# A four-stage kernel whose first stage is written out step by step, with the statistics and the application of each norm in different steps and scores ahead of projections

## The chip, the core and the metric

The kernel runs on one core of a Trainium2 chip. The time is the device time of one execution in microseconds (us). A core has five engines, each working through its own queue of instructions in order: TensorE (PE in the profile; its weight loads are listed as PEld), VectorE (DVE), ScalarE (ACT), GpSimd (POOL) and SyncE (SP, which here only issues transfers). They wait for one another by semaphores.

## What is computed

A sequence tensor x of 16 x 256 x 128 passes four residual blocks, each `x = x + LN(f(LN(x)))`. The change lies in the first one, windowed attention with sigmoid weights and 16 heads of 8:

```
x = x + _layernorm(_L0_attn_ref(_layernorm(x), wq, wkv, wo, gamma, beta))
x = x + _layernorm(_L0_ffn_ref(_layernorm(x), ...))      # attention over 16, experts
x = x + _layernorm(_L1_attn_ref(_layernorm(x), ...))     # state-space scan
x = x + _layernorm(_L1_ffn_ref(_layernorm(x), ...))      # gated ternary MLP

def _L0_attn_ref(x, wq, wkv, wo, gamma, beta):
    q = (x @ wq.T).reshape(B, T, H, HD)
    kv = (x @ wkv.T).reshape(B, T, H, 2 * HD)
    nb_k, nb_v = the 16 positions before each one
    tau = jax.nn.sigmoid(einsum('bthd,bthwd->bthw', q, nb_k) / SCALE)
    msg = einsum('bthw,bthwd->bthd', tau, nb_v)
    y = x + msg.reshape(B, T, D) @ wo.T
    return layernorm(y) * gamma + beta
```

## The kernel before

The four blocks run as stages a, b, c and d. Stage a takes the 16 sequences as 16 tiles of 256 tokens (two blocks of 128 tokens on the 128 partitions). Each engine runs `step_a(n, l, have)` for n from -2 to 16; in step n it works on several tiles at different points of their way, and `have(k)` tells whether tile n+k exists. Two sets of buffers (lanes, l = n % 2, o the other one) are used in turn, and the eight PSUM banks are four for each lane. `pipelined` (L81) writes out the first and last steps and makes a hardware loop of the twelve between them, two steps in one turn of the loop. The order of the work on each engine is the order in which `step_a` is written.

The way of one tile: DVE takes the statistics of x (`a_ln1.stats`, L109 and L112), POOL makes 1/sqrt(var+eps) of them (`rstd`, L118 and L119), DVE applies them (`apply`, L141, into t_xn). PE turns t_xn (`turn`, L1313), ACT rounds it to its high part xh (L645), DVE takes the rest as xl (L921). PE projects to q, k and v with nine matmuls of 256 columns (`project`, L1318 to L1320). ACT spreads k over four heads (hbd, L636) and copies q (mov, L652); DVE turns v and spreads it (vT and vbd, L925 and L926). PE makes the scores (L1353 lays the mask of the window, L1331 adds 32 products of 32 rows), ACT the sigmoid (tau, L657), PE the messages (L1370), ACT copies them (msgT, L664), and PE projects them out (L1337). DVE adds the residual (t_y, L948) and takes the statistics of a second norm (a_ln2) and applies it (t_zn); POOL scales and shifts it (L439, L440 into t_z); DVE takes the third norm's statistics of t_z (a_ln3) and applies it (t_o); POOL adds that to x (L465), and SP stores the tile to DRAM (L410).

In a step, PE has: project tile n+1, scores of tile n, turn tile n+2, wait for tau of tile n, its messages, wait for msgT, its outward projection. DVE has: t_y and the a_ln2 statistics of tile n-1; the a_ln1 statistics of tile n+2, a wait for POOL's `rstd` of it, its application; the application of a_ln2 (n-1); vT and vbd (n+1); the a_ln3 statistics of tile n-1, a wait for POOL's `rstd` of it, its application; and last xl of tile n+2, for which the next step's project waits.

Stage b starts when all 16 tiles are stored, and reads them back in another layout (L401). The constants and weights of all stages are loaded by ACT's queue at the start in four groups, a to d. All engines wait for group a; DVE then casts four constants, makes bqm and the high and low parts of the weights of stages a and b (`split`, L914 and L916), with a wait for group b before those of stage b, and only then begins stage a. What is printed below shows the functions that the change touches.

## Time and profile before

| | |
|---|---|
| median of 3 runs | 1067.92 us (1067.37, 1067.92, 1071.03) |
| the profiled execution | 1070.93 us |
| its span, first to last instruction | 1069.1 us |
| outside the span | 1.8 us |
| first scores of stage a (tile 0) | at 28.7 us |
| last scores of stage a (tile 15) | at 182.8 us |
| last addition of stage a | ends at 199.2 us |
| stages b, c and d | 199.2 to 1069.1 us |

The profile is of one execution. Its times are us from the first instruction unless ns stands there. A figure such as [1.09 <-POOL a_ln_rs L119] says that the engine stood idle for 1.09 us, and which instruction ended that. PEclk is TensorE's granted clock as a share of 2.4 GHz, so 0.50 is 1.2 GHz.

### The profile page before, as it was taken

Reading aid. Unit: us, or ns where it says so; the run is one execution under the profiler, and the core shown is the slowest. Engines: PE = TensorE matmul, PEld = TensorE weight load, DVE = VectorE, ACT = ScalarE, POOL = GpSimd, SP = SyncE. Lnnn points to the kernel's source line nnn. Section 1 sums busy time; section 2 is a strip of 40 time slices with the busy share of each in tenths; the row PEclk is TensorE's granted clock in tenths of the full one; section 3 lists DMA queues with packets and bytes.
Section 4 is the critical chain, followed back from the end, with each engine's and each line's share of the span. In section 5 each row is a group of like instructions: output and inputs, shape, how many; then the busy total and the mean of one; then the engine's idle time right before and its main releaser. Section 6 shows DMA issues by size and latency. Waiting matters only on the chain. (4 is left out here: it accounts for less than half of the span.)

```text
span 1069.1 us, 21886 instructions
## 1 busy us (share of the span) xinstructions
PE 876.1 (82%) x8256; PEld 721.9 (68%) x8256; DVE 683.1 (64%) x1966; ACT 556.9 (52%) x1049; POOL 460.7 (43%) x781
## 2 busy tenths in 40 slices
PE   1878777276999999998958778887669999999994
PEld 1767766265888888876745556665447878888783
DVE  3566665366588888865249999999965073370712
ACT  1434343133567667664657777778455263452630
POOL 1456565323255455434446777777660011020201
PEclk9855566555799989898878888778668999999997
DMA  9100000110000000000000000000000000000000
GB/s 311 37 12 13 15 10 17 40 50 1 2 2 2 2 2 2 2 2 1 1 1 1 1 1 1 1 1 2 1 0 1 1 1 21 1 20 1 11 11 20
DMA packets 22134, 16.55 MB, mean 15 GB/s; under 512 B 2576, under 2 KB 20376, under 8 KB 21792
## 3 DMA queue, kind: packets, MB, share of 16 engines
q1 hardware_dynamic: 17408, 8.39, 2.8%
q10 hardware_dynamic: 4640, 7.01, 1.8%
q8 instruction: 54, 0.88, 0.3%
q14 instruction: 32, 0.26, 0.1%
HBM read 11.20 MB, written 4.19 MB: 14 GB/s over the span
## 5 line engine op out<-in xcount | busy, mean ns | idle before, releaser
L118 POOL TENSOR_TENSOR d_ln_ve<-d_ln_mv,eps 128x4 f32<-128x4 f32 x16 | 3.2, 201 | 228.7 <-DVE d_ln_mv L112 228.7
L1319 PE MATMUL ps<-h_h,wh_l 128*128 128x512 f32 x256 | 99.7, 390 | 0.0
L1320 PE MATMUL ps<-h_l,wh_h 128*128 128x512 f32 x256 | 99.7, 390 | 0.0
L1318 PE MATMUL ps<-h_h,wh_h 128*128 128x512 f32 x256 | 99.7, 390 | 0.0
L1393 PE MATMUL ps<-w_e,he 128*128 128x128 f32 x512 | 87.7, 311 | 4.4 <-ACT he L676 4.0
L1331 PEld LDWEIGHTS ps<-mov,hbd 32*128 32x128 f32 x2048 | 85.2, 251 | 0.0
L1331 PE MATMUL ps<-mov,hbd 32*128 32x32 f32 (+1 forms) x2048 | 83.1, 325 | 0.0
L676 ACT ACTIVATE he<-ps,pp 128x256 f32<-128x256 f32 x128 | 59.5, 471 | 44.2 <-PE ps L1320 39.1
L1393 PEld LDWEIGHTS ps<-w_e,he 128*128 128x128 f32 x512 | 77.4, 222 | 7.0 <-ACT he L676 6.3
L1285 DVE TENSOR_TENSOR d_y<-ps,w_s 128x512 f32<-128x512 f32 x8 | 5.5, 691 | 103.0 <-PE ps L1711 103.0
L1251 DVE TENSOR_TENSOR h_l<-hid,h_h 128x512 fp32r<-128x512 f32 x64 | 48.5, 772 | 31.2 <-ACT h_h L883 30.3
L118 POOL TENSOR_TENSOR b_ln_ve<-b_ln_mv,eps 128x2 f32<-128x2 f32 x64 | 13.1, 204 | 107.8 <-DVE b_ln_mv L112 107.8
L1320 PEld LDWEIGHTS ps<-h_l,wh_h 128*128 128x128 f32 x256 | 48.1, 188 | 10.1
L1319 PEld LDWEIGHTS ps<-h_h,wh_l 128*128 128x128 f32 x256 | 48.1, 188 | 9.9
L1318 PEld LDWEIGHTS ps<-h_h,wh_h 128*128 128x128 f32 x256 | 48.1, 188 | 10.0
L1313 PE MATMUL ps<-ident,t_xn 128*128 128x128 f32 x64 | 18.4, 382 | 44.4 <-DVE t_xn L141 44.4
L887 ACT ACTIVATE hid<-ps,pp 128x512 f32<-128x512 f32 x32 | 22.1, 690 | 62.3 <-PE ps L1320 62.3
L1318 PE MATMUL ps<-hTh,we_h 128*128 128x256 f32 x128 | 53.8, 420 | 0.0
L636 ACT ACTIVATE hbd<-ps,headmask 128x256 f32<-128x256 f32 x64 | 25.1, 474 | 52.9 <-PE ps L1320 52.9
L1105 DVE TENSOR_TENSOR wall<-dec,wall 128x224 f32<-128x224 f32 (+6 forms) x112 | 47.8, 427 | 3.5
L545 POOL TENSOR_TENSOR term<-term 128x224 f32<-128x224 f32 (+2 forms) x48 | 35.4, 738 | 32.1 <-DVE term L1129 29.6
L119 POOL TENSOR_TENSOR b_ln_rs<-b_ln_ve,half 128x2 f32<-128x2 f32 x64 | 46.0, 718 | 5.0
(254 smaller groups left out, 2637.9 us busy)
## 6 DMA issues: line engine op xcount, KB each, us to landing
x<-in_x SPq DMA_DIRECT2D x16, 128.0 KB
w_h<-in_w_h ACTq DMA_DIRECT2D x2, 1024.0 KB, 7.8
x<-x SPq DMA_DIRECT2D x16, 128.0 KB, 1.8
xB<-x SPq DMA_DIRECT2D x32, 64.0 KB
out_x<-xB SPq DMA_DIRECT2D x32, 64.0 KB
w_m<-in_w_m ACTq DMA_DIRECT2D x3, 256.0 KB, 4.8
xB<-in_w_e ACTq DMA_DIRECT2D x1, 512.0 KB
w_e<-in_w_e ACTq DMA_DIRECT2D x1, 512.0 KB
```

What stands on the lines that cost most here:

```text
L119: pool.tensor_tensor(self.rs[l][:, :], self.ve[l][:, :], half[:, 0:self.k], ALU.pow).then_inc(self.rstd_ready, 1)
L545: chain.link(pool.tensor_tensor(y[:, :, j:CH], y[:, :, j:CH], wide[:, HALF - 1 - j, :, j:CH], ALU.add))
L636: last = act.activation(hbd[l][:, :, h, :], src, ACT.Copy, scale=headmask[:, h:h + 1])
L676: act.activation(he[e % 2][:, :], ps[:, HE + e % 2, 0:NT], ACT.Gelu, bias=vec("b1", e)).then_inc(he_ready, 1)
L887: act.activation(hid[l][:, m, :], bank(l, m), ACT.Gelu, scale=vec("h2_s", m)).then_inc(m_h2, 1)
L1105: ins = dve.tensor_tensor(wall[l][:, :, CH - 1 - j, j:CH], dec[l][:, 0, :, j:CH], wall[l][:, :, CH - j, j - 1:CH - 1], ALU.mult)
L1251: dve.tensor_tensor(dst[l][:, m, :], hid[l][:, m, :], high_part[l][:, m, :].bitcast(F32), ALU.subtract).then_inc(done, 1)
L1318: pe.matmul(dst, a_h, b_h, start=start, stop=True, skip_group_check=True)
L1319: pe.matmul(dst, a_l, b_h, start=False, stop=True, skip_group_check=True)
L1320: return pe.matmul(dst, a_h, b_l, start=False, stop=True, skip_group_check=True)
L1331: return pe.matmul(dst, hbd[l][heads(g), j, :, :].rearrange("p h s -> p (h s)"), mov[l][heads(g), BLK * j:BLK * j + w], start=False, stop= ...
L1393: last = pe.matmul(ps[:, ACC, P * c:P * c + P], he[e % 2][:, P * c:P * c + P], w_e2[:, e, :], start=False, stop=True, skip_group_check=True)
```

## The change

All of it concerns stage a and what lies ahead of it.

- The hardware loops of stage a on PE, ACT, DVE, POOL and SP are gone; the steps are written out, now from n = -3 to 17.
- PE: the scores of tile n stand ahead of the projection of tile n+1. The wait for xl of tile n+1 stands ahead of the scores too.
- DVE: the a_ln1 statistics are taken one step ahead of their application (for tile n+3), the a_ln3 application comes one step after its statistics (for tile n-2), and the a_ln2 application stands behind both.
- POOL: the copy of t_xn first, then `rstd` of a_ln2, the addition to x for tile n-2, scale and shift, `rstd` of a_ln1 and a_ln3 at the end.
- ACT: tau first, then hbd, xh, msgT and, last, mov.
- Group a of the loads is smaller: rows, same and negsel go to group b. DVE casts only band ahead of stage a, ACT casts rep. The splits of wf and w_e1, the casts of same and negsel, and bqm go to DVE's step 16, the wait for group b to the end of its step 14. POOL waits for group b in step 1. The Exp of log_A goes behind stage a on ACT.

```diff
-                  (wa[:, :, :], "wa"), (rows[:, :, :], "rows"), (pp[:, :], "pp")],
-            "b": [(wf[:, :, :], "wf"), ...
+                  (pp[:, :], "pp"), (wa[:, :, :], "wa")],
+            "b": [(rows[:, :, :], "rows"), (stage_f[2][:, :], "c_same"), (stage_f[3][:, :, :], "c_negsel"), (wf[:, :, :], "wf"), ...
...
 # POOL
-                if have(-1):
-                    a_ln2.rstd(pool, chain, eps, half, 1 - l, n)
-                if have(2):
-                    a_ln1.rstd(pool, chain, eps, half, l, n + 3)
...
+                if have(-2):
+                    pool.wait_ge(S["a_o"], n - 1)
+                    xt = x[:, 2 * n - 4:2 * n - 2, :]
+                    pool.tensor_tensor(xt, xt, t_o[l][:, :, :], ALU.add).then_inc(S["a_x"], 1)
...
+                    if n == 1:
+                        pool.wait_ge(w_loaded["b"], W_ALL["b"])
...
+                if have(3):
+                    a_ln1.rstd(pool, chain, eps, half, o, n + 4)
...
-            pipelined(pool, step_a, 2, 1, NB)
+            for n in range(-3, NB + 2):
+                step_a(n, n % 2, within(n))
...
 # DVE
+                if have(-2):
+                    a_ln3.apply(dve, lambda b: t_o[l][:, b, :], lambda b: t_z[l][:, b, :], l, n - 1).then_inc(S["a_o"], 1)
+                if n == NB:
+                    split(wf_h[:, :, :], wf_l[:, :, :], wf[:, 0:3, :], split_done, 2)
                 if have(-1):
                     a_ln2.apply(dve, lambda b: t_zn[o][:, b, :], lambda b: t_y[o][:, b, :], o, n).then_inc(S["a_zn"], 1)
+                if have(3):
+                    dve.wait_ge(x_loaded[o], 16 * ((n + 3) // 2 + 1))
+                    a_ln1.stats(dve, chain, lambda b: x[:, 2 * n + 6 + b, :], o)
+                if n == -3:
+                    split(wa_h[:, :, :], wa_l[:, :, :], wa[:, 0:3, :], split_done, 0)
+                if n == NB:
+                    split(we_h[:, :, :], we_l[:, :, :], w_e1[:, :, :], split_done, 4)
...
 # PE
-                if have(1):
-                    pe.wait_ge(S["a_xl"], n + 2)
-                    project(o, 4 * o, wa_h, wa_l, S["a_qk_ps"], S["a_v_ps"])
                 if have(0):
...
+                    if have(1):
+                        pe.wait_ge(S["a_xl"], n + 2)
...
+                if have(1):
+                    pe.wait_ge(S["a_xl"], n + 2)
+                    project(o, 4 * o, wa_h, wa_l, S["a_qk_ps"], S["a_v_ps"])
```

PE, a step in the middle of stage a, before (the last matmul of the projection, then the scores, the turn, the messages and the outward projection):

```order
L1320 MATMUL ps<-xl,wa_h 128x256
L1347 REGISTER_ALU
L1353 MATMUL ps<-band,rep 128x384 x4
L1331 MATMUL ps<-mov,hbd 128x48 x28
L1331 MATMUL ps<-mov,hbd 128x32 x4
L1363 REGISTER_ALU
L1311 REGISTER_ALU
L1313 MATMUL ps<-ident,t_xn 128x128 x2
L1366 ISA
L1370 MATMUL ps<-tau,vbd 32x48 x28
L1370 MATMUL ps<-tau,vbd 32x32 x4
L1337 MATMUL ps<-wa,msgT 128x128 x2
```

PE, the same step now:

```order
L1366 MATMUL ps<-band,rep 128x384 x4
L1344 MATMUL ps<-mov,hbd 128x48 x28
L1344 MATMUL ps<-mov,hbd 128x32 x4
L1331 MATMUL ps<-xh,wa_h 128x256
L1332 MATMUL ps<-xh,wa_l 128x256
L1333 MATMUL ps<-xl,wa_h 128x256
...
L1326 MATMUL ps<-ident,t_xn 128x128 x2
L1386 MATMUL ps<-tau,vbd 32x48 x28
L1386 MATMUL ps<-tau,vbd 32x32 x4
L1350 MATMUL ps<-wa,msgT 128x128 x2
```

The projection moved from ahead of the scores to between them and the turn, and so between the scores and the messages that wait for tau. The register instructions of the loop are gone.

DVE, a step in the middle of stage a, before (from the a_ln1 statistics on):

```order
L109 BN_STATS a_ln_st<-x 128x6
L112 BN_AGGR a_ln_mv<-a_ln_st 128x2 x2
L139 REGISTER_ALU
L141 TENSOR_SCALAR t_xn<-x,a_ln_mv,a_ln_rs 128x128 x2
L141 TENSOR_SCALAR t_zn<-t_y,a_ln_mv,a_ln_rs 128x128 x2
L925 STREAM_TRANSPOSE vT<-ps 128x256
L926 TENSOR_TENSOR vbd<-vT,vmask 128x1024
L109 BN_STATS a_ln_st<-t_z 128x6 x2
L112 BN_AGGR a_ln_mv<-a_ln_st 128x2 x2
L141 TENSOR_SCALAR t_o<-t_z,a_ln_mv,a_ln_rs 128x128 x2
L921 TENSOR_TENSOR xl<-ps,xh 128x256
```

DVE, the same step now (from the a_ln2 statistics on):

```order
L109 BN_STATS a_ln_st<-t_y 128x6 x2
L112 BN_AGGR a_ln_mv<-a_ln_st 128x2 x2
L141 TENSOR_SCALAR t_xn<-x,a_ln_mv,a_ln_rs 128x128 x2
L141 TENSOR_SCALAR t_o<-t_z,a_ln_mv,a_ln_rs 128x128 x2
L141 TENSOR_SCALAR t_zn<-t_y,a_ln_mv,a_ln_rs 128x128 x2
L109 BN_STATS a_ln_st<-x 128x6 x2
L112 BN_AGGR a_ln_mv<-a_ln_st 128x2 x2
L930 STREAM_TRANSPOSE vT<-ps 128x256
L931 TENSOR_TENSOR vbd<-vT,vmask 128x1024
L109 BN_STATS a_ln_st<-t_z 128x6 x2
L112 BN_AGGR a_ln_mv<-a_ln_st 128x2 x2
L926 TENSOR_TENSOR xl<-ps,xh 128x256
```

No application stands right behind its own statistics any more, and t_o no longer stands between vbd and xl.

DVE, the start of the program up to the first application of a norm, before:

```order
L914 CAST wa_h<-wa 128x384
L916 TENSOR_TENSOR wa_l<-wa,wa_h 128x384
L914 CAST wf_h<-wf 128x384
L916 TENSOR_TENSOR wf_l<-wf,wf_h 128x384
L914 CAST we_h<-xB 128x1024
L916 TENSOR_TENSOR we_l<-xB,we_h 128x1024
L56 ISA
L109 BN_STATS a_ln_st<-x 128x6 x2
L112 BN_AGGR a_ln_mv<-a_ln_st 128x2 x2
L141 TENSOR_SCALAR t_xn<-x,a_ln_mv,a_ln_rs 128x128 x2
```

DVE, the same place now:

```order
L915 CAST band<-stage_band 128x384
L56 ISA
L109 BN_STATS a_ln_st<-x 128x6 x2
L112 BN_AGGR a_ln_mv<-a_ln_st 128x2 x2
L919 CAST wa_h<-wa 128x384
L921 TENSOR_TENSOR wa_l<-wa,wa_h 128x384
L56 ISA
L141 TENSOR_SCALAR t_xn<-x,a_ln_mv,a_ln_rs 128x128 x2
```

The statistics of tile 0 moved ahead of all splits, and the splits of wf and w_e1 are no longer there.

## Rows read from the trace of the kernel before

**Rows 1.** Slices of 26.7 us: TensorE's busy tenths, granted clock in tenths

```profile
PE   1878777276999999998958778887669999999994
...
PEclk9855566555799989898878888778668999999997
```

**Rows 2.** By stretch: length, busy us (instructions) of PE, PEld, DVE, ACT, POOL; clock

```profile
28.71:182.79 154.08, 118.20 (x2195) 105.46 (x2194) 97.17 (x306) 60.81 (x134) 88.86 (x139) 0.65 0.05 16
182.79:199.21 16.42, 6.45 (x137) 5.88 (x136) 6.26 (x27) 1.90 (x3) 7.94 (x14) 0.50 0.05 14
199.21:1069.10 869.89, 745.58 (x5904) 606.01 (x5904) 568.34 (x1602) 489.66 (x902) 359.38 (x611) 0.85 0.02 6
101.91:112.45 10.54, 9.05 (x149) 8.17 (x149) 7.07 (x24) 4.01 (x10) 6.53 (x11) 0.50 0.04 12
143.23:153.85 10.62, 5.80 (x149) 4.93 (x149) 7.44 (x26) 4.33 (x11) 6.92 (x12) 0.95 0.01 2
```

**Rows 3.** Timeline, one step: start us, us, engine, line, what [idle before]

```profile
101.91 0.51 PE L1353 MATMUL ps<-band,rep 32*128 32x384 bf16 x4
...
105.60 0.69 PE L1313 MATMUL ps<-ident,t_xn 128*128 128x128 f32 x2
...
105.71 1.51 ACT L657 ACTIVATE tau<-ps 128x768 f32<-128x768 f32 x2 [2.50 <-PE ps L1331]
...
107.28 1.45 PE L1370 MATMUL ps<-tau,vbd 128*32 128x48 f32 x64 [0.99 <-ACT tau L657]
...
109.23 1.23 PE L1337 MATMUL ps<-wa,msgT 128*128 128x128 f32 x4 [0.50 <-ACT msgT L664]
...
110.22 0.58 PE L1318 MATMUL ps<-xh,wa_h 128*128 128x256 f32 x1
...
112.45 0.51 PE L1353 MATMUL ps<-band,rep 32*128 32x384 bf16 x4
```

**Rows 4.** Timeline of the same step, DVE and POOL

```profile
103.36 1.00 DVE L141 TENSOR_SCALAR t_xn<-x,a_ln_mv,a_ln_rs 128x128 f32 x2 [1.26 <-POOL a_ln_rs L119]
...
105.26 1.50 DVE L926 TENSOR_TENSOR vbd<-vT,vmask 128x1024 f32<-128x1024 f32 x1
...
105.76 1.58 POOL L440 TENSOR_TENSOR t_z<-t_zn,rows 128x256 f32<-128x256 f32 x1
...
109.23 0.60 DVE L141 TENSOR_SCALAR t_o<-t_z,a_ln_mv,a_ln_rs 128x128 f32<-128x128 f32 x2 [1.09 <-POOL a_ln_rs L119]
...
109.75 0.42 DVE L921 TENSOR_TENSOR xl<-ps,xh 128x256 fp32r<-128x256 f32 x1
```

**Rows 5.** Timeline, a step at the full clock

```profile
143.40 1.87 PE L1331 MATMUL ps<-mov,hbd 32*128 32x48 f32 x64
...
152.11 0.39 PE L1318 MATMUL ps<-xh,wa_h 128*128 128x256 f32 x1 [3.14 <-DVE xl L921]
```

**Rows 6.** Timeline, the start of the program and the first scores

```profile
10.32 0.23 DVE L909 CAST rep<-stage_rep 128x128 bf16<-128x128 f32 x1 [10.32 <-DMA pp<-in_pp]
...
14.84 0.36 DVE L914 CAST wf_h<-wf 128x384 fp32r<-128x384 f32 x1 [2.24 <-DMA iota<-in_c_iota]
...
17.57 0.48 DVE L109 BATCH_NORM_STATS2 a_ln_st<-x 128x6 f32<-128x128 f32 x2
...
28.71 0.51 PE L1353 MATMUL ps<-band,rep 32*128 32x384 bf16 x4
```

**Rows 7.** Timeline, the end of stage a behind the last outward projection

```profile
191.38 0.42 DVE L948 TENSOR_TENSOR t_y<-ps,t_xb 128x256 f32<-128x256 f32 x1 [1.46 <-PE ps L1337]
...
195.94 0.49 DVE L109 BATCH_NORM_STATS2 a_ln_st<-t_z 128x6 f32<-128x128 f32 x2 [1.64 <-POOL t_z L440]
...
197.81 0.60 DVE L141 TENSOR_SCALAR t_o<-t_z,a_ln_mv,a_ln_rs 128x128 f32<-128x128 f32 x2 [1.09 <-POOL a_ln_rs L119]
...
198.49 0.72 POOL L465 TENSOR_TENSOR x<-x,t_o 128x256 f32<-128x256 f32 x1 [0.72 <-DVE t_o L141]
```

**Rows 8.** Instruction queue: packets, MB, share of 16 DMA engines

```profile
q8 instruction: 54, 0.88, 0.3%
```

More of the change, by code:

```diff
@@ L406, in _ @@
             load(1, 0, load_seq(a["x"]))
-            with sp.Fori(0, ITER) as i:
-                for l in LANES:
-                    sp.wait_ge(S["a_x"], i * 2 + l + 1)
-                    sp.dma_start(by_seq(x1)[bass.ds(i * 4 + 2 * l, 2)].rearrange("b p d -> p b d"),
-                                 x[:, bass.ds(i * 4 + 2 * l, 2), :]).then_inc(S["a_stored"], 16)
+            for t in range(NB):
+                sp.wait_ge(S["a_x"], t + 1)
+                sp.dma_start(by_seq(x1)[2 * t:2 * t + 2].rearrange("b p d -> p b d"),
+                             x[:, 2 * t:2 * t + 2, :]).then_inc(S["a_stored"], 16)
             sp.wait_ge(S["a_stored"], 16 * NB)
@@ L457, in step_a @@
                         pool.wait_ge(S["a_y"], n)
-                    copy(t_xb[1 - l][:, :, :], t_xn[1 - l][:, :, :], ones[:, :].unsqueeze(1).to_broadcast([P, 2, D])
+                    copy(t_xb[o][:, :, :], t_xn[o][:, :, :], ones[:, :].unsqueeze(1).to_broadcast([P, 2, D])
                          ).then_inc(S["a_xb"], 1)
                 if have(-1):
-                    scale_shift(1 - l, n, S["a_zn"], t_zn, t_zn, t_z, 0, 1, S["a_z"])
-                    a_ln3.rstd(pool, chain, eps, half, 1 - l, n)
-                    pool.wait_ge(S["a_o"], n)
-                    xt = x[:, bass.ds(n * 2 - 2, 2), :]
-                    pool.tensor_tensor(xt, xt, t_o[1 - l][:, :, :], ALU.add).then_inc(S["a_x"], 1)
-            pipelined(pool, step_a, 2, 1, NB)
+                    a_ln2.rstd(pool, chain, eps, half, o, n)
+                if have(-2):
+                    pool.wait_ge(S["a_o"], n - 1)
+                    xt = x[:, 2 * n - 4:2 * n - 2, :]
+                    pool.tensor_tensor(xt, xt, t_o[l][:, :, :], ALU.add).then_inc(S["a_x"], 1)
+                if have(-1):
+                    if n == 1:
+                        pool.wait_ge(w_loaded["b"], W_ALL["b"])
+                    scale_shift(o, n, S["a_zn"], t_zn, t_zn, t_z, 0, 1, S["a_z"])
+                if have(3):
+                    a_ln1.rstd(pool, chain, eps, half, o, n + 4)
+                if have(-1):
+                    a_ln3.rstd(pool, chain, eps, half, o, n)
+            for n in range(-3, NB + 2):
+                step_a(n, n % 2, within(n))
             def step_b(n, q, have):
@@ L664, in step_a @@
                     act.activation(msgT[l][:, :], bank(l, 0, 0, NT), ACT.Copy).then_inc(S["a_msgT"], 1)
+                if have(1):
+                    act.activation(mov[o][:, :], ps[:, 4 * o, 0:NT], ACT.Copy).then_inc(S["a_qT"], 1)
             act.wait_ge(w_loaded["a"], W_ALL["a"])
+            act.activation(rep[:, :], stage_f[0][:, :], ACT.Copy).then_inc(cast_ready, 1)
+            for n in range(-3, NB + 2):
+                step_a(n, n % 2, within(n))
             act.activation(expA[:, :], vec("log_A"), ACT.Exp).then_inc(expA_ready, 1)
-            pipelined(act, step_a, 2, 1, NB)
             def gelu(n, l, e):
@@ L906, in _ @@
             dve.wait_ge(w_loaded["a"], W_ALL["a"])
[L907 to L910 removed]
+            dve.tensor_copy(band[:, :], stage_f[1][:, :]).then_inc(cast_ready, 1)
             def split(dst_h, dst_l, src, done, before):
@@ L970, in step_a @@
                     a_ln3.stats(dve, chain, lambda b: t_z[o][:, b, :], o)
-                    a_ln3.apply(dve, lambda b: t_o[o][:, b, :], lambda b: t_z[o][:, b, :], o, n).then_inc(S["a_o"], 1)
+                if n == NB:
+                    for dst, src in ((same[:, :], stage_f[2][:, :]), (negsel[:, :, :], stage_f[3][:, :, :])):
+                        dve.tensor_copy(dst, src).then_inc(cast_ready, 1)
+                    dve.tensor_scalar(bqm[:, :], headmask[:, :], vec("bq"), None, ALU.mult).then_inc(cast_ready, 1)
                 if have(2):
                     low_part(l, 4 * o + 3, n + 3, S["a_xh"], S["a_xl"])
-            split(wa_h[:, :, :], wa_l[:, :, :], wa[:, 0:3, :], split_done, 0)
-            dve.wait_ge(w_loaded["b"], W_ALL["b"])
-            split(wf_h[:, :, :], wf_l[:, :, :], wf[:, 0:3, :], split_done, 2)
-            split(we_h[:, :, :], we_l[:, :, :], w_e1[:, :, :], split_done, 4)
-            pipelined(dve, step_a, 2, 1, NB)
+                if n == NB - 2:
+                    dve.wait_ge(w_loaded["b"], W_ALL["b"])
+            for n in range(-3, NB + 2):
+                step_a(n, n % 2, within(n))
             def step_b(n, q, have):
@@ L1375, in step_a @@
                     out_tokens(4 * l + 3, msgT[l], wa[:, 3, :], S["a_y_ps"])
-            pe.wait_ge(split_done, 4)
-            pipelined(pe, step_a, 2, 1, NB)
+            pe.wait_ge(split_done, 2)
+            for n in range(-3, NB + 2):
+                step_a(n, n % 2, within(n))
             def up(n, q, e):
```

35 lines of the change are left out of this document (14 added, 21 removed).

## The prediction

> **What bounds the kernel now.** I read the busy share by slice first, then the busy times by stretch, and then one step of stage a in order of time. Stage a is slices 2 to 8 of 40: TensorE is busy for seven or eight tenths of them, and for most of them its clock is granted at 5 to 7 tenths [rows 1]. From the first scores to the last it takes 154.1 us, that is 15 step-to-step distances of 10.3 us on average, with a mean clock of 0.65; what lies behind it takes 869.9 us and isn't touched [rows 2]. Since the clock has two levels (1.0 of full and 0.5), 0.65 means about 30% of the time at 2.4 GHz; the part behind, at 0.85, has 70%.
>
> In the step from 101.91 to 112.45 (1.2 GHz, 10.54 us) TensorE is the busiest engine and still has two holes: it waits 0.99 us for tau and 0.50 us for msgT, because both are made from what it has just finished, and only the turn of 0.69 us stands between scores and messages [rows 3]. VectorE is busy for 7.07 us of the same step, and it stands idle twice for a reciprocal root that GpSimd makes of statistics VectorE has only just taken: 1.26 us ahead of t_xn and 1.09 us ahead of t_o; xl comes last, ends at 110.17, and the projection starts at 110.22 [rows 3, 4]. So two chains of nearly the same length bound the step. At 2.4 GHz this shows best: the step at 143.23 has TensorE busy for only 5.80 of 10.62 us and is no shorter, and the projection waits 3.14 us for xl [rows 2, 5]. VectorE's chain alone gives 10.4 us whatever TensorE's clock is. A change that shortened only one of the two chains would gain little. This one goes at both.
>
> **Part 1, TensorE's step.** The rows give the pieces at 1.2 GHz: scores 105.60 − 101.91 = 3.69, projection 112.45 − 110.22 = 2.23, turn 0.69, messages with the wait for msgT 109.23 − 107.28 = 1.95, outward projection 110.22 − 109.23 = 0.99 [rows 3]. Now the projection stands between scores and messages. Tau takes 1.51 us from the end of the scores [rows 3]; projection and turn are 2.92 us, so the 0.99 us wait for it goes. The msgT wait stays: nothing was put there. Sum: 3.69 + 2.23 + 0.69 + 1.95 + 0.99 = **9.55 us**; 0.1 us of the last piece is the wait for xl in this step, so 9.5 us.
>
> **Part 2, VectorE's chain.** Statistics of x are taken a step ahead, t_o a step behind, and between the a_ln2 statistics and t_zn now stand t_xn and t_o, some 1.2 us of work against a wait of 1.1 to 1.3 us: all three waits for GpSimd are covered [rows 4]. What is left is the work, 7.1 us (6.5 if vbd runs apart from GpSimd's t_z: 1.50 and 1.58 us side by side here [rows 4]; 97.17/15 = 6.5 is the mean [rows 2]). But there is a new order to check: vT and vbd need v, which comes out only when the projection ends, at 3.69 + 2.23 + 0.2 = 6.1 us of the step. Behind it VectorE has vT (0.5), vbd (1.2 to 1.5), the a_ln3 statistics (0.8) and xl (0.45), after which the next scores may start: 9.1 to 9.4 us. This is just under TensorE's 9.5, so at 1.2 GHz TensorE sets the step by a hair. At 2.4 GHz its scores take 1.87 + 0.17 us [rows 5] and the projection half of 2.23, the same chain starts at 3.4 us but VectorE is only then through with its first five pieces, and the step is VectorE's own work plus small gaps: **7.3 us**. ScalarE (tau 1.51, hbd 1.6, three copies of 0.4 = 4.3 us) and GpSimd (6.5 to 6.9 us busy a step [rows 2]) have room in either case; ScalarE's mov is last, but it runs beside the outward projection.
>
> **Part 3, the share of steps at either clock.** The trace can't decide this, so I bound it: all steps at 1.2 GHz give 9.5 us a step, all at 2.4 GHz 7.3. Stage a had 30% so far, the stages behind have 70% with TensorE 86% busy (745.6/869.9) [rows 2]. In the new step TensorE is 94% busy at the low clock and some 68% at the high one, more than before (86% and 55%). The mix of matmuls is stage a's own, so I stay nearer to its 30% and take 40%: 0.6 x 9.5 + 0.4 x 7.3 = 8.62 us, times 15 = **129.3 us** from the first scores to the last, against 154.1.
>
> The Trainium skill, "TensorE: Matmul & The Clock Gate", Part 1, says that sustained activity of TensorE brings the full clock and an idle window takes it away. By that rule the clock ought to have been high in stage a already, and would be now, which is the third rival below. The trace doesn't bear it out so far: a step with 9.05 of 10.54 us busy runs at 0.50 throughout [rows 2].
>
> **Part 4, the start.** Before, group a lands at 10.32 us, group b at 14.84, the splits end at 17.57, where the first statistics start, and the first scores come at 28.71 [rows 6]. Those 11.1 us hold two projections of 2.23; the second now comes behind the first scores, leaving 8.9. Group a shrinks from about 1220 to 612 KB (from the shapes), its last load is issued seventh instead of tenth; halving the time from the first landing at about 2 us gives 6.0, the time of issue adds up to 1, so group a lands at 7.0 (between 6 and 9). Casting band takes 0.4, the first statistics start at 7.4, the first scores at **16.3 us**. The wa split (0.9) lies in the wait for the first root. Group b is now waited for in GpSimd's step 1, near 25 us, ten us after it lands.
>
> **Part 5, the end.** From the last scores to the end of stage a are 16.4 us [rows 2]. The splits of 0.9 and 1.9 us and casts of 1.2 stand in VectorE's last full step. Ahead of them stands t_o of tile 14 (0.6). The wait for a root (1.1) covers t_o and half of the first split, the wait for t_z (1.64) nearly all of the second, the last wait (1.09) nearly all of the casts [rows 7]. I add **1.0 us** (0.5 to 2): 17.4.
>
> **Part 6, at nothing.** The loop's register and branch instructions go; they lay between waits. Written-out code must be fetched: 54 packets took 0.3% of 16 x 1069.1 us, 0.95 us each [rows 8], and a step of TensorE is about one packet, beside a step of 8 us: hidden. The store of each tile is issued as before.
>
> **Sum.** 16.3 + 129.3 + 17.4 = 163.0 us for the end of stage a, against 199.2: 36.2 us less. Span 1069.1 − 36.2 = 1032.9, the profiled execution 1034.7; that execution lies 3.0 above the median of 1067.92, from which the same step gives **1031.7 us**; I say 1032.
>
> **The rivals.** *The clock stays low all through.* 15 x 9.5 = 142.5, end of stage a at 176.2, gain 23.0: 1045 us. For it speaks that busy steps ran at 0.50 before. *The clock is high all through* (the skill's rule above): 15 x 7.3 = 109.5, gain 56: 1012 us. Against it speaks the mean of 0.65. *The steps gain nothing*, because a chain that I place wrongly (VectorE behind the projection, or GpSimd's longer queue ahead of t_z) takes up what the two others give: 15 x 10.4 = 156, end at 189.7, only the start is won: 1058 us. It is decided by 1.0 us more in a chain that I have at 9.1 to 9.4. *The change doesn't do what it says*: the waits are renamed, and the start hangs on the transfers of x instead; then within 0.5%. I see no row for it. *Slower: the written-out code starves TensorE.* The loop's twelve steps needed no fetching, now all do, the first of them while the transfers fill the queues. It takes over 36.2/15 = 2.4 us of fetching a step that nothing hides, more than two packets at 0.95, to lose what the rest wins; at 3 us a step 1032 + 45 = 1077 us. Stages b to d are written out already and TensorE is busy for 86% of them, which speaks against it [rows 2].
>
> **How the numbers follow.** Forecast (1022 to 1040) 50%, clock low 25%, clock high 10%, steps gain nothing 9%, no effect 3%, slower 3%. The range of 8 in 10 takes the forecast, the low clock with 7 us for a late start and a dear end (1052), and goes down to the high clock (1012), half of which is out. A difference under 0.5% (5.3 us) can't be told from none here. Faster by more: 50 + 25 + 10 + 9 = 94%; the same 3%; slower 3%.
>
> **What the profile after would show.** Part 1 is right if messages no longer wait for tau; part 2 if no application waits over 0.3 us for GpSimd in full steps, and xl is followed by scores within 0.3 us at 2.4 GHz; part 3 by the distance between scores, 9.5 and 7.3 at the two clocks, and the mean clock of the stretch, 0.70; part 4 by first scores at 16.3; part 5 by 17.4 from the last scores to the last addition. Scores 10 us apart, or an idle TensorE with no releaser, would make it wrong.

## The result, and the profile after

| kernel | median us | lowest to highest | runs |
|---|---|---|---|
| before | 1068.35 | 1067.37 to 1071.03 | 4 |
| after | 1032.83 | 1029.47 to 1038.13 | 4 |

The ratio is 0.967, with a 95% interval of 0.9645 to 0.9691: the kernel is 35.5 us faster. The profiled execution of after is the one of 1038.13 us, with a span of 1036.3.

**Slices.** The page of after cuts its span into 40 slices (25.9 us each): busy tenths of TensorE, then its granted clock in tenths.

```profile
PE   1888882669999999988777778987479999999994
...
PEclk9985665557899999888888888788679999999997
```

**Stretches.** The columns are those of [rows 2]: the stretch, its length, then busy us (instructions) of PE, PEld, DVE, ACT and POOL, the granted clock, the share of the DMA engines and GB/s. The first line goes from the first scores to the last, the second from there to the last addition of stage a, the third covers all the rest. The last three are single steps of stage a: the first of all, one at the low and one at the high clock.

```profile
25.84:148.47 122.63, 106.91 (x2203) 97.14 (x2203) 92.22 (x302) 59.46 (x135) 80.56 (x135) 0.76 0.09 25
148.47:165.60 17.13, 4.73 (x137) 4.18 (x136) 11.86 (x40) 3.38 (x5) 11.59 (x17) 0.57 0.06 17
165.60:1036.30 870.70, 745.43 (x5904) 605.60 (x5904) 569.00 (x1602) 489.12 (x901) 359.86 (x612) 0.85 0.02 6
25.84:35.29 9.45, 8.95 (x148) 8.19 (x149) 3.02 (x9) 4.60 (x10) 0.89 (x2) 1.00 0.40 117
90.16:99.61 9.45, 8.95 (x149) 8.19 (x149) 6.48 (x22) 4.02 (x9) 5.56 (x10) 0.50 0.06 16
108.47:115.61 7.14, 5.10 (x148) 4.55 (x148) 6.86 (x23) 3.79 (x9) 6.40 (x11) 1.00 0.07 21
```

Stage a's fifteen steps take 122.6 us instead of 154.1, its end 17.1 instead of 16.4, and the untouched rest 870.7 instead of 869.9 [rows 2]. The first scores come at 25.84 us; before it was 28.71 [rows 6]. So 31.5 us come from the steps and only 2.9 from the start. At the low clock TensorE is busy for 8.95 of 9.45 us. At the high clock it has 2 us to spare and VectorE is busy for 6.86 of 7.14.

The clock that is printed for the start of a trace can't be taken as it stands. The first step, 25.84 to 35.29, is printed with 1.00, and yet TensorE is busy for 8.95 of its 9.45 us, exactly as in the step at 0.50, and its first matmuls (the mask) take 0.51 us, as at 99.61 below, and not 0.34, as at 108.47. The trace has records of the clock only from 41.6 us on (in before from 40.1), and the time ahead of the first one is counted as full, although the matmuls there take as long as at 1.2 GHz. With that time counted as 0.50, the mean of the stretch is 0.70 in after and not 0.76, and in before 0.61 and not 0.65. These, and the others called corrected below, are estimates from the traces.

**A step in order of time.** Start (us), length (us), engine, line, what, and in brackets the idle time before and what ended it. These are the rows of after that answer to [rows 3 to 5]: the end of a step that begins at the low clock, and then the one at the high clock.

```profile
99.61 0.51 PE L1366 MATMUL ps<-band,rep 32*128 32x384 bf16 x4
...
103.30 0.58 PE L1331 MATMUL ps<-xh,wa_h 128*128 128x256 f32 x1
103.41 1.51 ACT L658 ACTIVATE tau<-ps 128x768 f32<-128x768 f32 x2 [4.74 <-PE ps L1344]
...
105.94 1.06 PE L1386 MATMUL ps<-tau,vbd 128*32 128x48 f32 x64
...
108.47 0.34 PE L1366 MATMUL ps<-band,rep 32*128 32x384 bf16 x4 [0.23 <-DVE xl L926]
...
109.42 0.68 DVE L141 TENSOR_SCALAR t_xn<-x,a_ln_mv,a_ln_rs 128x128 f32<-128x128 f32 x2
...
110.02 0.59 DVE L141 TENSOR_SCALAR t_o<-t_z,a_ln_mv,a_ln_rs 128x128 f32<-128x128 f32 x2
...
110.69 0.74 POOL L461 TENSOR_TENSOR x<-x,t_o 128x256 f32<-128x256 f32 x1
110.72 1.06 DVE L141 TENSOR_SCALAR t_zn<-t_y,a_ln_mv,a_ln_rs 128x128 f32<-128x128 f32 x2
...
112.67 0.73 POOL L439 TENSOR_TENSOR t_z<-t_zn,rows 128x256 f32<-128x256 f32 x1
112.82 1.66 DVE L931 TENSOR_TENSOR vbd<-vT,vmask 128x1024 f32<-128x1024 f32 x1
113.35 1.18 POOL L118 TENSOR_TENSOR a_ln_ve<-a_ln_mv,eps 128x2 f32<-128x2 f32 x1
...
115.07 0.39 DVE L926 TENSOR_TENSOR xl<-ps,xh 128x256 fp32r<-128x256 f32 x1
...
115.61 0.34 PE L1366 MATMUL ps<-band,rep 32*128 32x384 bf16 x4 [0.78 <-DVE xl L926]
```

The messages at 105.94 have no bracket: the projection stands over tau, and the 0.99 us of [rows 3] is gone. t_xn, t_o and t_zn follow one another without a wait for GpSimd, where [rows 4] has 1.26 and 1.09 us. And the last xl (115.07 + 0.39) is followed by the scores within 0.15 us. At the full clock TensorE has a hole of 0.78 us there, so VectorE sets the step.

**The start.** The same view from 0 us on; `ACTq` is the issue of a load from ScalarE's queue. It answers to [rows 6].

```profile
6.95 0.36 DVE L915 CAST band<-stage_band 128x384 bf16<-128x384 f32 x1 [6.95 <-DMA wa<-in_wa]
...
7.23 0.48 DVE L109 BATCH_NORM_STATS2 a_ln_st<-x 128x6 f32<-128x128 f32 x2
...
9.43 0.60 DVE L141 TENSOR_SCALAR t_xn<-x,a_ln_mv,a_ln_rs 128x128 f32<-128x128 f32 x2 [0.60 <-POOL a_ln_rs L119]
...
17.38 0.61 ACTq L633 DMA_DIRECT2D w_s<-in_w_s  x1
...
18.02 1.28 ACT L673 ACT_TABLE_LOAD   x1 [18.02 <-issue]
...
19.32 0.31 ACT L673 ACTIVATE rep<-stage_rep 128x128 bf16<-128x128 f32 x1
...
19.73 0.66 PE L1326 MATMUL ps<-ident,t_xn 128*128 128x128 f32 x2 [19.73 <-ACT rep L673]
...
20.84 0.42 DVE L926 TENSOR_TENSOR xl<-ps,xh 128x256 fp32r<-128x256 f32 x1 [10.14 <-ACT xh L649]
...
25.84 0.51 PE L1366 MATMUL ps<-band,rep 32*128 32x384 bf16 x4 [1.80 <-DVE xl L926]
```

Group a lands at 6.95 us and the statistics start at 7.23, both as forecast. But ScalarE issues the loads of all four groups, until 18 us. Only then come its table load and the cast of rep, which TensorE's first turn waits for, and behind that xh. VectorE stands idle for 10.14 us.

### The profile page after: what moved, and what is told of

The parts are those of the page before. It is cut to its first block and busy times, and to the rows that moved or that the text cites. A ratio compares the mean times of both kernels' runs of the same rounds, so it can differ in the third digit from the quotient of the medians.

```text
span 1036.3 us, 21603 instructions
## 1 busy us (share of the span) xinstructions
PE 860.4 (83%) x8256; PEld 709.6 (68%) x8256; DVE 679.9 (66%) x1965; ACT 556.8 (54%) x1050; POOL 457.0 (44%) x781
## 3 DMA queue, kind: packets, MB, share of 16 engines
q8 instruction: 65, 1.06, 0.5%
## 5 line engine op out<-in xcount | busy, mean ns | idle before, releaser
L1344 PEld LDWEIGHTS ps<-mov,hbd 32*128 32x128 f32 x2048 | 82.1, 242 | 0.0
L1344 PE MATMUL ps<-mov,hbd 32*128 32x32 f32 (+1 forms) x2048 | 80.7, 317 | 0.0
L658 ACT ACTIVATE tau<-ps 128x768 f32<-128x768 f32 x32 | 24.2, 809 | 59.9 <-PE ps L1344 59.9
```

The costliest lines, as they stand in the source:

```text
L658: act.activation(tau[l][:, 2 * k:2 * k + 2, :], ps[:, 4 * l + 2 * k:4 * l + 2 * k + 2, 0:NBLK * SPAN], ACT.Sigmoid, scale=ATT_SCALE).then_ ...
L1344: return pe.matmul(dst, hbd[l][heads(g), j, :, :].rearrange("p h s -> p (h s)"), mov[l][heads(g), BLK * j:BLK * j + w], start=False, stop= ...
```

## The experiments

Every kernel below is after with the edit shown. "Stretch" is from the first scores to the last, fifteen steps. A median is of 4 runs or more, a ratio is to the kernel before on the same chip, with its 95% interval. Where the gain came from is asked first, then what the start and the other engines hold back.

### The moved loads and the written-out code alone: all_orders_old

The orders inside a step are put back on all four engines. The smaller group a, the moved splits and the written-out steps stay.

```diff
 # PE
+                if have(1):
+                    pe.wait_ge(S["a_xl"], n + 2)
+                    project(o, 4 * o, wa_h, wa_l, S["a_qk_ps"], S["a_v_ps"])
                 if have(0):
                     pe.wait_ge(S["a_qT"], n + 1)
...
-                    project(o, 4 * o, wa_h, wa_l, S["a_qk_ps"], S["a_v_ps"])
 # ACT: hbd, mov, tau, xh, msgT (was tau, hbd, xh, msgT, mov)
 # DVE, POOL: as in norms_old below
```

> The changed kernel with the order inside a step put back on all engines: the first stage stays written out, and the loads, casts and splits stay where the change put them. Theory (the gain is in the steps, since ScalarE issues loads until 18.0 us in the changed kernel and then only casts rep and copies xh): first scores at 28 us, 10.3 us from scores to scores, an end dearer by 1 us, 1068 us in all. Rival (the moved loads and the written-out code carry a good part of the gain): 1058 us or less.

Measured: 1069.33 us (1065.58 to 1072.35), ratio 1.0005 (0.9992 to 1.0019). First scores 27.80, steps of 10.16 us on average, 18.55 us from the last scores to the end of stage a, span 1070.6. The theory held. The start is 0.9 us earlier and the end 2.1 us longer. The moved loads and splits and the written-out code together neither give nor cost anything that can be measured; no run has one without the other. Nearly the whole gain therefore hangs on the orders.

### One chain at a time: norms_old and pe_act_old

In norms_old PE and ACT keep the new order, and the norms on DVE and POOL are as before.

```diff
 # POOL
+                if have(-1):
+                    a_ln2.rstd(pool, chain, eps, half, o, n)
+                if have(2):
+                    a_ln1.rstd(pool, chain, eps, half, l, n + 3)
...
                 if have(-1):
-                    a_ln2.rstd(pool, chain, eps, half, o, n)
-                if have(-2):
-                    pool.wait_ge(S["a_o"], n - 1)
-                    xt = x[:, 2 * n - 4:2 * n - 2, :]
-                    pool.tensor_tensor(xt, xt, t_o[l][:, :, :], ALU.add).then_inc(S["a_x"], 1)
...
-                if have(3):
-                    a_ln1.rstd(pool, chain, eps, half, o, n + 4)
...
+                    pool.wait_ge(S["a_o"], n)
+                    xt = x[:, 2 * n - 2:2 * n, :]
+                    pool.tensor_tensor(xt, xt, t_o[o][:, :, :], ALU.add).then_inc(S["a_x"], 1)
 # DVE (the a_ln1 statistics go back to tile n+2, ahead of their application)
-                if have(-2):
-                    a_ln3.apply(dve, lambda b: t_o[l][:, b, :], lambda b: t_z[l][:, b, :], l, n - 1).then_inc(S["a_o"], 1)
...
+                if have(-1):
+                    a_ln3.apply(dve, lambda b: t_o[o][:, b, :], lambda b: t_z[o][:, b, :], o, n).then_inc(S["a_o"], 1)
                 if have(2):
                     low_part(l, 4 * o + 3, n + 3, S["a_xh"], S["a_xl"])
```

> The changed kernel with the orders of VectorE and GpSimd as before: scores ahead of projections alone. Theory (two chains, and the projection's new place makes v late for VectorE, which still waits for two roots behind it): 6.1 us for v, then 0.5 + 1.5 + 0.8 + 1.1 + 0.6 + 0.45 gives 11.0 us and more a step at 1.2 GHz, 10.2 at 2.4 GHz, so 8 to 12 us slower than all orders old, 1076 to 1080 us. Rival (TensorE alone bounds the step): 9.5 us a step at 1.2 GHz, 1050 us.

In pe_act_old it is the other way round: the norms are new, the projection is ahead of the scores again and tau behind hbd and mov.

> The changed kernel with the orders of TensorE and ScalarE as before: only the norms' statistics and applications apart. Theory (VectorE no longer bounds, TensorE keeps its wait for tau): 10.4 us a step at 1.2 GHz, 7.2 at 2.4 GHz, with half the steps at each 8.8, so 1042 to 1046 us, that is two thirds of the gain. Rival (both halves are needed, neither gives anything alone): 10.3 us at either clock, 1068 us.

| orders | median us | ratio | mean step | clock of the stretch, printed (corrected) | end of stage a |
|---|---|---|---|---|---|
| both old (all_orders_old) | 1069.33 | 1.0005 (0.9992 to 1.0019) | 10.16 | 0.67 (0.63) | 198.74 |
| PE and ACT new (norms_old) | 1067.28 | 0.9981 (0.9968 to 0.9995) | 10.18 | 0.73 (0.57) | 196.51 |
| norms new (pe_act_old) | 1046.67 | 0.9797 (0.9777 to 0.9817) | 8.32 | 0.79 (0.75) | 171.26 |
| both new (after) | 1032.83 | 0.9668 (0.9645 to 0.9691) | 8.18 | 0.76 (0.70) | 165.60 |

The norms alone give 22.7 us, the projection alone 2.1, both together 36.5: behind the new norms, the projection is worth 13.8. So there are two chains, and VectorE's was the longer one. pe_act_old came out 0.7 us above the 1042 to 1046 of my theory, with its steps of 10.4 and about 7 us. norms_old did not: neither 1076 to 1080 nor the rival's 1050. (Its 0.73 is mostly the unrecorded start: its matmuls stay at their low-clock lengths until 75 us.) The rows that decide it are two steps of norms_old, in order of time.

```profile
59.34 0.93 DVE L141 TENSOR_SCALAR t_xn<-x,a_ln_mv,a_ln_rs 128x128 f32<-128x128 f32 x2 [1.46 <-POOL a_ln_rs L119]
...
60.18 0.59 DVE L141 TENSOR_SCALAR t_zn<-t_y,a_ln_mv,a_ln_rs 128x128 f32<-128x128 f32 x2
...
62.58 1.46 PE L1384 MATMUL ps<-tau,vbd 128*32 128x48 f32 x64
62.74 1.23 DVE L930 TENSOR_TENSOR vbd<-vT,vmask 128x1024 f32<-128x1024 f32 x1
...
65.74 0.60 DVE L141 TENSOR_SCALAR t_o<-t_z,a_ln_mv,a_ln_rs 128x128 f32<-128x128 f32 x2 [1.10 <-POOL a_ln_rs L119]
...
66.83 0.51 PE L1364 MATMUL ps<-band,rep 32*128 32x384 bf16 x4 [1.07 <-DVE xl L925]
...
77.41 0.34 PE L1364 MATMUL ps<-band,rep 32*128 32x384 bf16 x4 [1.49 <-DVE xl L925]
```

The messages no longer wait for tau, as in after. But the scores wait for xl for 1.07 and 1.49 us: TensorE's hole has moved, from ahead of the messages to ahead of the scores, and the step stays at 10.58. It is 0.4 us shorter than the 11.0 that I had; more than half of that is vbd, which now runs apart from GpSimd's t_z and takes 1.23 us, not the 1.50 of [rows 4].

pe_act_old shows the opposite half. The first line is a message step at the high clock, the second at the low one:

```profile
65.63 0.86 PE L1382 MATMUL ps<-tau,vbd 128*32 128x48 f32 x64 [1.24 <-ACT tau L662]
...
75.33 1.45 PE L1382 MATMUL ps<-tau,vbd 128*32 128x48 f32 x64 [0.99 <-ACT tau L662]
```

TensorE still waits for tau, 13 times between 30 and 140 us. At the low clock its step is up to 10.4 us. At the high one it is 6.8 to 6.9, but the next one then takes longer (6.93 and 7.98 from 55.05 to 69.96), so that two together take 14.9 us, where VectorE is busy for 14.2. In the profiled executions the projection's new place gives 5.7 us up to the end of stage a: 1.8 at the start (27.67 to 25.84), 2.1 in the stretch, at a lower clock than pe_act_old's, and 1.7 at the end (18.84 to 17.13). The medians are 13.8 apart. Of the other 8 us, 5.3 are that after's profile is the longest of its four runs, and 2.9 lie in the stages b to d (873.6 and 870.7 us), which neither edit touches. So how much of the 13.8 is the projection's is not shown to better than some us.

### ScalarE's queue of loads: loads_on_sp and rep_on_dve

In loads_on_sp SyncE issues the groups c and d, behind the first loads of x.

```diff
 # ACT
-            for part in "abcd":
+            for part in "ab":
...
 # SP
             load(1, 0, load_seq(a["x"]))
+            for part in "cd":
+                for dst, name in loads[part]:
+                    sp.dma_start(dst, a[name]).then_inc(w_loaded[part], 16)
```

> The changed kernel, with the loads of groups c and d issued by SyncE behind its loads of x, and not by ScalarE ahead of its first step. Theory (the start hangs on ScalarE's queue of loads): rep and the first xh at 10 to 11 us in place of 19.3 and 20.4, first scores at 16 to 17 us in place of 25.8, 9 us less, 1024 us. Rival (the transfers themselves hold the start, by the landing of x): first scores within 2 us of 25.8, no change.

Measured: 1019.98 us (1018.57 to 1026.48), ratio 0.9559 (0.9518 to 0.9600), 4 us below the 1024 of the theory. First scores at 16.75; the profiled stretch is 8.9 us shorter than after's as well (113.71). The start in order of time:

```profile
8.46 0.45 ACTq L636 DMA_DIRECT2D iota<-in_c_iota  x1
8.94 1.28 ACT L676 ACT_TABLE_LOAD   x1 [8.94 <-issue]
10.24 0.31 ACT L676 ACTIVATE rep<-stage_rep 128x128 bf16<-128x128 f32 x1
10.64 0.66 PE L1329 MATMUL ps<-ident,t_xn 128*128 128x128 f32 x2 [10.64 <-ACT rep L676]
11.34 0.38 ACT L652 ACTIVATE xh<-ps 128x256 fp32r<-128x256 f32 x1 [0.80 <-PE ps L1329]
```

The table load comes 9.1 us earlier and so do the first scores. The 16.3 that I had forecast for the change is nearly what this kernel does. The shorter stretch isn't shown to come from this edit: rep_on_dve, next, has after's loads and steps and a stretch of 112.02.

In rep_on_dve only the cast of rep goes back to VectorE, and ScalarE keeps its loads.

```diff
-            act.activation(rep[:, :], stage_f[0][:, :], ACT.Copy).then_inc(cast_ready, 1)
...
             dve.tensor_copy(band[:, :], stage_f[1][:, :]).then_inc(cast_ready, 1)
+            dve.tensor_copy(rep[:, :], stage_f[0][:, :]).then_inc(cast_ready, 1)
```

> The changed kernel, with only the cast of rep given back to VectorE. Theory (ScalarE's whole queue stands behind its loads, the first xh too): the first turn moves up to 10 us, but the first xh only from 20.4 to 19.3 us, so 1 us less at the most. Rival (it is the cast on ScalarE alone that holds the start): first scores at 16 to 17 us, 9 us less.

Measured: 1030.25 us (1022.02 to 1031.41), ratio 0.9615 (0.9564 to 0.9667).

```profile
10.81 0.66 PE L1326 MATMUL ps<-ident,t_xn 128*128 128x128 f32 x2 [10.81 <-DVE t_xn L141]
...
17.27 1.28 ACT L649 ACT_TABLE_LOAD   x1 [17.27 <-issue]
18.57 0.38 ACT L649 ACTIVATE xh<-ps 128x256 fp32r<-128x256 f32 x1
...
23.98 0.51 PE L1366 MATMUL ps<-band,rep 32*128 32x384 bf16 x4 [1.80 <-DVE xl L926]
```

The turn comes 9 us earlier, and xh and the first scores less than 2 (1.9, where I had said 1 at the most). The dependence on rep was only the first thing to fall behind ScalarE's queue; everything ScalarE does is behind it. Of the two causes, the queue is the one. The profiled stretch of rep_on_dve is 10.6 us shorter than after's, with the same order in every step and a clock of 0.85 (corrected 0.81) against 0.76 (0.70), while the medians are 2.6 us apart: two executions can differ by that much in the share of the high clock.

### Less work for VectorE: sp_and_act, sp_act_turn, sp_act_root, all_in

VectorE sets the high-clock step, so I moved the application of a_ln3 (0.59 us a step) to ScalarE, which is busy for only half of the stretch. GpSimd makes one more two-element value for it, in two operations.

```diff
 # sp_and_act: loads_on_sp, and
 # POOL
-                    a_ln3.rstd(pool, chain, eps, half, o, n)
+                    a_ln3.rstd_and_shift(pool, chain, eps, half, minus, o, n)
 # DVE
-                if have(-2):
-                    a_ln3.apply(dve, lambda b: t_o[l][:, b, :], lambda b: t_z[l][:, b, :], l, n - 1).then_inc(S["a_o"], 1)
 # ACT, ahead of tau
+                if have(-2):
+                    a_ln3.apply_act(act, lambda b: t_o[l][:, b, :], lambda b: t_z[l][:, b, :], l, n - 1).then_inc(S["a_o"], 1)
```

> Groups c and d issued by SyncE, and the application of the third norm (t_o) by ScalarE in place of VectorE, with two small GpSimd operations more. Theory (VectorE's own work sets the step at 2.4 GHz, TensorE's at 1.2): 6.5 to 6.7 us in place of 7.15 at the high clock, 9.45 unchanged at the low one, 3 to 4 us less than loads on SyncE alone. Rival (GpSimd or ScalarE is as near to the bound as VectorE): 7.1 to 7.3 us at the high clock, no gain.

Measured: 1026.10 us, ratio 0.9597 (0.9569 to 0.9626): 6 us more than loads_on_sp, not 3 to 4 less. The waits of VectorE from 30 to 140 us: engine, what waited, for what, us in total, times, longest. The first fence is loads_on_sp, the second sp_and_act.

```profile
...
DVE t_zn L141 <- POOL a_ln_rs L119: 1.2, 2, 0.6
```

```profile
DVE t_zn L141 <- POOL a_ln_rs L119: 17.1, 14, 1.8
```

VectorE's busy time in the stretch fell from 94.26 to 87.19 us, so 7 us of work are gone. But t_o was what stood over GpSimd's root of a_ln2. Without it t_zn waits for that root in nearly every step, 17.1 us in total where it was 1.2, and the steps at 1.00 from 50 us on are 7.5 to 7.7 us instead of 7.1 to 7.3. I estimate that t_o had covered about half of these 16 us (14 times 0.59); the other half is GpSimd's two new operations, which stand ahead of the root and take about 0.5 us a step. The work that was moved away had been hiding a wait of its own size, and the move made the wait longer.

sp_act_turn also puts the turn of tile n+2, and xh with it, behind the messages and msgT:

```diff
 # PE
-                    turn(4 * o + 3, t_xn[l], 2, S["a_xn"], n + 3, S["a_t_ps"])
...
                     last.then_inc(S["a_m_ps"], 1)
+                    turn(4 * o + 3, t_xn[l], 2, S["a_xn"], n + 3, S["a_t_ps"])
                     pe.wait_ge(S["a_msgT"], n + 1)
 # ACT: msgT ahead of xh
```

> As the one before, and the turn of tile n+2 put behind the messages, where TensorE waits 0.5 us for msgT. Theory (at 1.2 GHz TensorE's work and its waits set the step): 8.95 us in place of 9.45 at the low clock, unchanged at the high one, 2 to 4 us less. Rival (xh and xl come too late then, VectorE's chain behind the projection takes over at once): 9.4 us or more, no gain.

Measured: 1024.71 us, ratio 0.9591 (0.9563 to 0.9619), 1.4 us less, in the right direction and within the noise of the two.

sp_act_root is sp_and_act with GpSimd's root of a_ln2 ahead of its copy of t_xn:

```diff
 # POOL
+                if have(-1):
+                    a_ln2.rstd(pool, chain, eps, half, o, n)
                 if have(1):
...
                     copy(t_xb[o][:, :, :], ...).then_inc(S["a_xb"], 1)
-                if have(-1):
-                    a_ln2.rstd(pool, chain, eps, half, o, n)
```

> t_o on ScalarE as in the run that lost 6 us to loads on SyncE alone, but GpSimd makes the second norm's root ahead of its copy of t_xn. Theory (that run lost because two more GpSimd operations stood ahead of this root, for which t_zn waited 0.88 us and more): the wait ahead of t_zn falls to 0.3 us or less, high steps 6.7 to 7.0 us, 3 to 6 us less than that run, 1020 to 1023 us. Rival (it lost by the share of the high clock or on ScalarE): the wait falls and the steps stay at 7.5 to 7.9 us.

Measured: 1024.65 us, ratio 0.9586 (0.9549 to 0.9622). VectorE's waits from 30 to 140 us again:

```profile
DVE t_zn L141 <- POOL a_ln_rs L119: 11.3, 14, 1.4
```

The copy was a third of the wait and not all of it, so my expectation of 0.3 us a step fell, and with it the 6.7 to 7.0 us a step: the high-clock steps are 7.5 to 7.7 as before. The two new operations still stand ahead of the root, and only t_xn is left over it.

all_in joins loads_on_sp, rep on VectorE, the late turn, t_o on ScalarE and the early root.

> All together: loads of c and d on SyncE, rep cast by VectorE, turn behind the messages, t_o on ScalarE, second root ahead of the copy. Theory: first scores at 16 us, low steps 8.9 us, high steps 6.7 to 7.0, 1014 to 1018 us, the fastest. Rival (the parts take from one another): 1020 us or more.

Measured: 1023.96 us, ratio 0.9588 (0.9553 to 0.9622), which is the rival's side: the parts take from one another. It is 8 us above sp_turn below, whose main difference is that it leaves t_o on VectorE and GpSimd without the two operations for it.

### The late turn alone: sp_turn

loads_on_sp, with the turn and xh moved as in sp_act_turn; t_o stays on VectorE.

> Loads on SyncE, and the turn of tile n+2 behind the messages, with t_o left on VectorE. Theory: 8.95 us in place of 9.45 at the low clock, 7.2 unchanged at the high one, where VectorE's work sets the step; with two thirds of the steps high 2 us less than loads on SyncE alone. Rival (xl comes later in high steps too): over 7.4 us there, and no gain.

Measured: 1015.81 us (1014.57 to 1017.05), ratio 0.9506 (0.9472 to 0.9541): 4 us less than loads_on_sp, and no run of the one reaches into those of the other, though the intervals of the ratios overlap. Its steps are 7.19 us in seven of fifteen cases. The turn stands where TensorE waited for msgT: from 30 to 140 us these waits fall from 12.0 to 4.9 us. At the high clock VectorE has the last word again: the scores wait 1.0 to 1.1 us for xl.

### More work for TensorE: sp_out_twice and sp_turn_twice

The printed clock of the stretch was 0.65 before, 0.76 after, 0.79 to 0.86 in most kernels above. To see whether TensorE's work or its holes set it, both kernels make the two matmuls of the outward projection (four in the records of the trace) twice, with the same output; sp_out_twice from loads_on_sp, sp_turn_twice from sp_turn.

```diff
+                    for c in range(2):
+                        pe.matmul(ps[:, 4 * l + 3, P * c:P * c + P], msgT[l][:, P * c:P * c + P], wa[:, 3, :], start=True, stop=True)
                     out_tokens(4 * l + 3, msgT[l], wa[:, 3, :], S["a_y_ps"])
```

> Loads on SyncE, with the outward projection of every tile made twice, the second over the first: the same output, 0.9 us of TensorE work more a step at 1.2 GHz, 0.4 to 0.7 at 2.4. Theory (TensorE sets the step at 1.2 GHz alone): 10.3 us in place of 9.45 in low steps, 7.2 unchanged in high ones, 3 to 6 us slower at the same share of high steps. Rival (the added activity raises the clock's share so far that it pays): mean clock of the stage over 0.9 and no loss against loads on SyncE.

> Loads on SyncE, the turn behind the messages, and the outward projection made twice, the second over the first. Theory (the added work costs nothing in high steps, where VectorE sets the step, and keeps the clock up): mean clock of the stage 0.9 or more, as in the run with the projection twice (0.94), no more than two steps of 15 over 8.5 us, 1013 to 1016 us. Rival (the 0.94 was the luck of one execution): clock 0.82 to 0.87, low steps of 9.4 us, 1017 us or more.

The stretch in loads_on_sp, then sp_out_twice, then sp_turn_twice, in the columns of [rows 2]:

```profile
16.75:130.46 113.71, 94.53 (x2204) 85.33 (x2205) 94.26 (x304) 58.80 (x135) 84.52 (x137) 0.84 0.21 65
```

```profile
16.76:129.29 112.53, 92.09 (x2263) 83.61 (x2264) 95.31 (x304) 57.82 (x135) 85.88 (x135) 0.94 0.21 66
```

```profile
17.38:128.65 111.27, 92.64 (x2263) 82.32 (x2264) 95.88 (x304) 57.71 (x135) 86.92 (x135) 0.95 0.21 68
```

Measured: sp_out_twice 1019.06 us (1018.91 to 1019.83), ratio 0.9543 (0.9509 to 0.9577); sp_turn_twice 1014.61 us (1013.44 to 1017.90), ratio 0.9491 (0.9478 to 0.9504). For sp_out_twice the rival came true, not the theory that had the doubled work cost 3 to 6 us in all; for sp_turn_twice the theory did. TensorE has more instructions and a higher clock, and the step does not grow. Corrected for the start, the three clocks are 0.80, 0.90 and 0.92. They aren't the luck of one execution: the mean clock of the whole run is 0.860 to 0.863 in all four runs of sp_out_twice, against 0.841 to 0.852 in loads_on_sp, and 0.863 to 0.869 in the five of sp_turn_twice, against 0.855 to 0.858 in sp_turn. Whether the added work does it by its amount or by where it stands, no run tells. The three stretches also show how little is left in the clock: at 0.94 the mean step is 7.50 us and at 0.84 it was 7.58, because at either value most steps are VectorE's. sp_turn_twice has the lowest median of all, but its runs overlap with sp_turn's; the doubling isn't shown to be worth anything there.

## Why the prediction was right, and where not

I had said 1032 us, between 1012 and 1052; it is 1032.83. That closeness is partly luck: two terms were off by 7 to 10 us, in opposite directions. The sum was for the profiled execution, with 1034.7, and that took 1038.13.

| term | forecast | measured |
|---|---|---|
| first scores | 16.3 | 25.84 |
| low-clock step | 9.5 | 9.45 |
| high-clock step | 7.3 | 7.14 |
| mean clock of the stretch | 0.70 | 0.76 printed, 0.70 corrected |
| fifteen steps | 129.3 | 122.63 |
| last scores to end of stage a | 17.4 | 17.13 |
| end of stage a | 163.0 | 165.60 |
| the rest | 869.9 | 870.7 |

**Part 1** was right: at the low clock tau (1.51 us) lies under the projection and the turn, which take 2.64 us from 103.30 to the messages at 105.94, no wait is left, and the msgT wait is still there. At the high clock they just suffice: tau ends at 112.06 and the messages start at 112.11.

**Part 2** was right in its mechanism (but for "all three waits": [rows 4] has two): in full steps no application waits for GpSimd, but for t_zn once between 30 and 140 us, by 0.6, and the high-clock step is VectorE's own work plus small gaps. Within the sum, t_zn grew from 0.59 us (its row in norms_old) to 1.06 beside GpSimd's addition to x, and vbd, at the high clock, from 1.23 to 1.66 beside t_z. They used up part of what the waits gave back. norms_old and pe_act_old show the claim of two chains: either edit alone gives 2 or 23 us, and both 36.5.

**Part 3** was mis-sized, and not in the clock. I took 40% of the stretch at the high clock, a mean of 0.70. The printed 0.76 would be 52%, but corrected for the start it is 0.70, and my "30% so far" is 22% by the same count: I had read the 0.65 of before as it was printed. What I had wrong is the length of the steps at a given clock. Each step's length set against 9.5 and 7.3 us weighed by its own clock gives this estimate of the 6.7 us. Some 1.6 are the share, 45% when each step counts alike. 1.3 are the last step, which has no projection and no turn any more and takes 6.02 us. Some 3.2 are the steps with both clocks in them, six of the seven shorter than the straight line between my two values: the one from 67.09 to 74.37 has 0.77 and takes 7.28 us, where the line gives 8.3. The little that is left are steps at one clock, just under my values. TensorE's busy time falls from 8.95 to 5.10 us between the two clocks, well below VectorE's 6.86, so a part of a step at the high clock is enough to bring TensorE down to where VectorE sets the length.

I had stayed near the 30% of before "since the mix of matmuls is stage a's own". sp_out_twice shows that the share isn't bound to that mix so closely: 60 more matmul records on 2204 take the printed clock from 0.84 to 0.94. Nor does the busy share alone decide it. TensorE is busy for 8.95 of 9.45 us at 0.50 in one step of after and for 5.10 of 7.14 at 1.00 in another. The Trainium skill, "TensorE: Matmul & The Clock Gate", Part 1, has sustained activity bring the full clock. By that rule the first of the two steps should have had it, and the page was named for the rival of a high clock throughout (1012 us; the second of the rivals, not the third, as I had counted it); after's trace doesn't agree. rep_on_dve has the same steps as after and 0.85 in its profiled execution where after has 0.76, so part of the difference between two kernels is one between two executions. What sets the share stays open.

**Part 4** is the step that failed: of the 12.4 us that it gave to the start, 9.5 didn't come. "Group a lands at 7.0" and "statistics at 7.4" were right to 0.2 us. But from there I followed VectorE and TensorE alone and gave no time to ScalarE, which makes xh and, since the change, rep. It had all the loads to issue first: some 0.45 us each, until 18.0. So the first xh starts at 20.43, where before it started at 20.88; the rest of the 2.9 us is the second projection, which now stands behind the first scores. The trace of before could have told me: there ScalarE's table load starts at 17.44 us, behind the same 32 rows of load issues. It just didn't matter, because the splits on VectorE ended as late, ahead of the statistics at 17.57 [rows 6]. The change removed one of two delays of the same length. loads_on_sp removes the other and gets 16.75, and rep_on_dve excludes that the cast of rep alone held the start.

**Part 5.** The 1.0 us that I added for the splits was 0.7 (17.13 against 16.42). **Part 6** held: the instruction queue has grown as follows, from [rows 8], and all_orders_old, which has the written-out steps too, is at 1.0005.

```profile
q8 instruction: 65, 1.06, 0.5%
```

Of the rivals, the steps that gain nothing came near in norms_old, where one of the two chains was left as it was. Written-out code that starves TensorE shows in no row.

The best kernel of the study is sp_turn: after with SyncE issuing groups c and d and the turn behind the messages, 1015.8 us, 4.9% under the kernel before and 1.6% under after.

## What to carry to other kernels

Where two engines' chains are nearly of a length, an edit of one alone gives almost nothing (2 us here), and the same edit after the other 14: cost both before judging either. When a start is made earlier, follow every engine that the first result passes through, with all that its queue holds ahead of it, loads that it issues for later stages included. Before work is moved off the bounding engine, look for the wait that it covers: t_o left VectorE, and a wait of twice its length came in its place, half of it by the operations that the move had added. And read the clock of a stretch against the lengths of the matmuls in it: here the first 6 to 50 us of the stretch were printed at a clock that they didn't have.
